# Counters set one stage ahead, batch 0's scores ahead of its layer norm, and a third of the slot table's lanes on ScalarE

## The reference

```python
x = x + xattn(layernorm(x), ctx)       # q, k = ctx @ Wq.T + bq, ctx @ Wk.T + bk
                                       # x + layernorm(x) mixed over channels by softmax(q k^T)
def ffn(x):                            # of layernorm(x); 4 batches of 512 tokens, width 512
    h = rmsnorm(x, ln1_w)
    x = x + causal_attention(h) @ wo   # 16 heads of 128
    h = rmsnorm(x, ln2_w)
    p = softmax(h @ gate_w.T)          # 16 experts, the 6 best of each token, weights made to sum to 1
    return x + routed(h, p) + shared(h)   # silu(h @ g) * (h @ u) @ d, width 352, shared 704
```

## Time and profile before

| | |
|---|---|
| runs, us | 2218.95, 2215.73, 2219.56 (median 2218.95) |
| profiled execution, us | 2220.62 |
| its span, first to last instruction | 2218.8 |
| PE busy | 2126.3 (96%) |
| DVE, POOL, ACT busy | 1146.1, 983.3, 699.4 |
| mean granted clock of PE | 0.985 |

### The profile page before, as it was taken

How to read it: one execution, slowest core, us unless ns; L and a number is a source line. 1 busy time by engine, 2 the same in 40 slices (tenths; PEclk the granted TensorE clock), 3 DMA queues, 4 the chain that set the end, 5 groups by cost and what they waited for, 6 DMA issues and landing times. The chain is left out here.

```text
span 2218.8 us, 39627 instructions
## 1 busy us (share of the span) xinstructions
PE 2126.3 (96%) x11850; PEld 1857.6 (84%) x11851; DVE 1146.1 (52%) x2520; ACT 699.4 (32%) x1832; POOL 983.3 (44%) x1036
## 2 busy tenths in 40 slices
PE   7899999999999999999996998889999999999997
PEld 5788888988888898888874876679999999999996
DVE  6746556464655646465566476633333333433332
ACT  6634334343433434343444211112222222222221
POOL 2535454545545454554515025534444444444442
PEclk9999999999999999999997999999999999999998
DMA  2214343443433344343415111086776776677443
GB/s 105 95 58 162 125 141 119 153 153 113 161 126 138 121 154 151 113 165 124 147 53 223 77 67 48 20 270 160 194 202 159 190 203 162 161 197 199 81 77 52
DMA packets 140690, 300.62 MB, mean 135 GB/s; under 512 B 16800, under 2 KB 16800, under 8 KB 138592
## 3 DMA queue, kind: packets, MB, share of 16 engines
q1 hardware_dynamic: 115392, 241.26, 30.6%
q0 software_dynamic: 24960, 58.21, 13.3%
q10 hardware_dynamic: 288, 0.53, 0.1%
HBM read 177.51 MB, written 122.42 MB: 135 GB/s over the span
## 5 line engine op out<-in xcount | busy, mean ns | idle before, releaser
L1094 POOL TENSOR_TENSOR chunk_hi<-chunk_raw,zero 128x512 fp32r<-128x512 f32 x153 | 159.3, 1041 | 239.9 <-DMA chunk_raw<-in_whole 239.9
L1975 POOL DMA_INDIRECT out<-y,sidx x111 | 177.4, 1598 | 62.8 <-issue 41.2
L1096 POOL TENSOR_TENSOR chunk_raw<-chunk_raw,chunk_hi 128x512 fp32r<-128x512 f32 x153 | 197.7, 1292 | 12.0
L1312 DVE TENSOR_TENSOR pT_lo<-ps,pT_hi 128x384 fp32r<-128x384 f32 (+2 forms) x256 | 111.2, 456 | 176.7 <-ACT pT_hi L1253 172.8
L2125 DVE TENSOR_TENSOR prod<-ps,silu 128x352 f32<-128x352 f32 x111 | 58.3, 525 | 271.6 <-PE ps L69 242.6
L1284 DVE SCALAR_TENSOR_TENSOR HS<-ps,rinv,HS 128x512 f32<-128x512 f32 x260 | 176.9, 743 | 2.8 <-PE ps L69 2.8
L1982 POOL TENSOR_TENSOR carry<-ident 128x1 f32<-128x1 f32 x214 | 42.6, 199 | 300.9 <-DVE gidx L2131 210.3
L1242 ACT ACTIVATE prob<-ps,negmax 128x512 f32<-128x512 f32 (+3 forms) x256 | 131.7, 527 | 110.1 <-DVE negmax L1273 110.1
L2120 DVE TENSOR_SCALAR y<-ps,weight_of 128x512 f32<-128x512 f32 x111 | 83.3, 751 | 136.3 <-PE ps L69 132.6
L67 PE MATMUL ps<-wv_or_qk_hi,hT_hi 128*128 128x256 f32 x512 | 146.4, 286 | 5.0 <-POOLq L1104 5.0
L67 PE MATMUL ps<-ring,xT_0hi 128*128 x448 | 150.2, 335 | 0.8 <-DMA ring<-split_weights 0.8
(11 more groups left out here) (320 smaller groups left out, 6064.7 us busy)
## 6 DMA issues: line engine op xcount, KB each, us to landing
ring<-split_weights SPq DMA_DIRECT2D x240, 272.0 KB
chunk_raw<-in_whole SPq DMA_DIRECT2D x153, 256.0 KB, 2.7
split_weights<-chunk_hi SPq DMA_DIRECT2D x153, 256.0 KB, 2.4
split_weights<-chunk_raw SPq DMA_DIRECT2D x153, 256.0 KB, 2.6
xg<-in_wqk SPq DMA_DIRECT2D x16, 512.0 KB, 3.6
x_spill<-x SPq DMA_DIRECT2D x4, 1024.0 KB, 4.1
xg<-in_wv SPq DMA_DIRECT2D x8, 512.0 KB, 3.4
xg<-in_wo SPq DMA_DIRECT2D x8, 512.0 KB, 5.1
```

Source lines behind the costliest of these rows:

```text
L1094: nc.gpsimd.tensor_tensor(chunk_hi[k][:], chunk_raw[k][:], zero[:].to_broadcast([P, CH]), ALU.add).then_inc(chunk_high, 1)
L1096: nc.gpsimd.tensor_tensor(chunk_raw[k][:].bitcast(F32R), chunk_raw[k][:], chunk_hi[k][:].bitcast(F32), ALU.subtract).then_inc(chunk_low, 1)
L1312: nc.vector.tensor_tensor(pT[1][:, 0:split, w], ps_t[k % 2][:, 0:split * P].rearrange("p (j t) -> p j t", t=P), pT[0][:, 0:split, w].bitca ...
L1975: nc.gpsimd.indirect_dma_start(out, bass.IndirectOffsetOnAxis(ap=sidx[q][:], axis=0), y[q][:], None, bounds_check=T + P - 1, oob_is_err=Tr ...
```

## The change

It does four things.

- The counters of `self_attention` (28 increments, `EARLY` and the three raised by 2 among them) are counted up by POOL at the start of `cross_attention`, and those of `routed_experts` (14) in `shared_expert`, between POOL's set-up and its wait for the packed slots. The first waits for `pool_0` of PE, ACT and DVE in `self_attention` and of PE in `routed_experts` are gone.
- In batch 0 of `cross_attention` PE makes the scores before it turns x, ACT takes queries and keys out of PSUM and splits the next features before it norms x, and copies the turned x between exponents and probabilities. Queries and keys of batch 1 wait for `dve_qk` instead of the four exponents, and x's tiles have other PSUM banks.
- The third lane of each batch is made by ACT in two instructions (`Abs` of lane minus count, then `Relu` of 1 minus that), at the end of each slot. PE waits for it with one wait more.
- In the slots c = 0 to 2 DVE makes the first column of a batch between `prod` and the low part, except for batch 0.

The earlier, unused copies of functions are deleted, which moves line numbers.

```diff
+            for counter in following:            # cross_attention, POOL, before of_x(0)
+                nc.gpsimd.sem_inc(counter, ONE)
+            for counter in following[0:2]:
+                nc.gpsimd.sem_inc(counter, EARLY)
+            for counter in following[2:5]:
+                nc.gpsimd.sem_inc(counter, 2)
             of_x(0)
...
-        banks = {("x", 0): B + C_, ("e", 0): D_ + A}
+        banks = {("e", 0): B + C_, ("x", 0): D_ + B}
...
-                    if n < 3:
+                    if n == 1:
+                        pe.wait_ge(dve_qk, 2)
+                    elif n == 2:
                         pe.wait_ge(act_exp, ST * n)
...
             keys_and_queries(0)
+            scores(0)
             normed_x(0)
-            scores(0)
...
             act.wait_ge(ld_b, 32)
+            high_qk1(0)
+            high_feat(1)
             layer_norm(0)
-            high_qk1(0)
-            high_of_tiles(columns(xT[0]), "x", 0)
             for n in range(NB):
-                if n + 1 < NB:
+                if 0 < n < NB - 1:
                     high_feat(n + 1)
...
-                softmax(n)
+                exponents(n)
+                if n == 0:
+                    high_of_tiles(columns(xT[0]), "x", 0)
+                probabilities(n)
...
             low_qk1(0)
-            low_of_tiles(*both(xT), "x", 0)
...
                 if n == 0:
+                    low_of_tiles(*both(xT), "x", 0)
                     statistics(1)
...
-            for counter in counters:             # self_attention and routed_experts, POOL
-                nc.gpsimd.sem_inc(counter, ONE)
...
-            pe.wait_ge(pool_0, 1)                # the same for act and dve
...
+            for counter in following:            # shared_expert, POOL
+                nc.gpsimd.sem_inc(counter, ONE)
             pool.wait_ge(dve_r, PACKED)
...
-                for b in range(RING):
+                for b in range(RING - 1):
                     r, t = divmod(RING * k + b, TT)
                     nc.gpsimd.tensor_scalar(in_lane[b][:], count[:], lane[:, t, r:r + 1], None, ALU.is_equal).then_inc(pool_lane, 1)
...
-                pe.wait_ge(pool_lane, RING * (k + 1))
+                pe.wait_ge(pool_lane, (RING - 1) * (k + 1))
+                pe.wait_ge(act_lane, 2 * (k + 1))
...
+            def last_lane(n, slot):
...
+                apart = in_lane[RING - 1]
+                nc.scalar.activation(apart[:], count[:], ACT.Abs, bias=lane[:, t, r:r + 1], scale=-1.0).then_inc(act_lane, 1)
+                act.wait_ge(act_lane, 2 * k + 1)
+                nc.scalar.activation(apart[:], apart[:].bitcast(F32), ACT.Relu, bias=1.0, scale=-1.0).then_inc(act_lane, 1)
...
+            ahead = lambda n, c: 1 if at_slot.get((n, c), 0) else 0
...
+                    columns(n, c, range(ahead(n, c)))
                     dve.wait_ge(act_h, q + 1)
...
-                    columns(n, c)
+                    columns(n, c, range(ahead(n, c), RING))
```

More of the change, by code:

```diff
@@ L124, in _ @@
                                     pattern=[[-1, P]], channel_multiplier=1).then_inc(made, 1)
-def high_qk(nc, qkT, corner, m, bank):
-    w, scale = slice(P if m == 0 else 0, S), SCALE if m == 0 else 1.0
-    nc.scalar.mul(corner[:, m, :], bank[:, 0:P], scale)
-    return nc.scalar.mul(qkT[0][:, m, w], bank[:, w], scale)
-def low_qk(nc, qkT, m, bank):
-    w = slice(P if m == 0 else 0, S)
-    return nc.vector.scalar_tensor_tensor(out=qkT[1][:, m, w], in0=bank[:, w], scalar=SCALE if m == 0 else 1.0,
-                                          in1=qkT[0][:, m, w].bitcast(F32), op0=ALU.mult, op1=ALU.subtract)
@@ L730, in attention @@
                     pe.wait_ge(act_nrm, ST * n + i + 1)
-                    if i == 0 and n >= 2:
+                    if n == 0:
+                        pe.wait_ge(dve_t, tile("x", 0) + i + 1)
+                    elif i == 0 and n >= 2:
                         pe.wait_ge(dve_t, tile("h", n - 2) + ST)
@@ L843, in softmax, with probabilities @@
                                          accum_out=rsum[:, i:i + 1]).then_inc(act_exp, 1)
+            def probabilities(n):
                 for i in range(ST):
@@ L996, in self_attention @@
         sb = lambda name, shape, dt=F32: ctx.enter_context(nc.sbuf_tensor(name, shape, dt))
-        counters, count = counting(sem)
         at = placing(nc, slab)
@@ L1713, in _ @@
         def _(act):
+            def last_lane(n, slot):
+                k = at_slot.get((n, slot))
+                if k is None:
+                    return
+                r, t = divmod(RING * k + RING - 1, TT)
+                if k == 0:
+                    act.wait_ge(dve_r, PACKED)
+                else:
+                    act.wait_ge(pe_table, k)
+                apart = in_lane[RING - 1]
+                nc.scalar.activation(apart[:], count[:], ACT.Abs, bias=lane[:, t, r:r + 1], scale=-1.0).then_inc(act_lane, 1)
+                act.wait_ge(act_lane, 2 * k + 1)
+                nc.scalar.activation(apart[:], apart[:].bitcast(F32), ACT.Relu, bias=1.0, scale=-1.0).then_inc(act_lane, 1)
             act.wait_ge(dve_r, LOGITS)
@@ L1731, in _ @@
                     nc.scalar.copy(hh[n % 2][0][0:w, c, :], prod[0:w, :]).then_inc(act_h, 1)
+                    last_lane(n, c)
+                if n >= 1:
+                    for i in range(ST):
+                        last_lane(n, NI + i)
         @block.vector
@@ L1837, in unit_tables, with columns @@
                 nc.vector.tensor_copy(base_of[:], ps_unit[:, 1, 0:UNITS])
-            def columns(n, slot):
+            def columns(n, slot, some=range(RING)):
                 k = at_slot.get((n, slot))
@@ L1847, in columns @@
                     dve.wait_ge(pe_table, k)
-                for b in range(RING):
+                for b in some:
                     r, t = divmod(RING * k + b, TT)
```

399 lines of the change are left out of this document (37 added, 362 removed).

## The result

The changed kernel takes 2204.43 us (median of 4 runs, 2203.29 to 2205.18) against 2219.26 of the kernel before beside it: ratio 0.9935, interval 0.9918 to 0.9952, or 14.8 us less where 13.4 were forecast. The profiled execution took 2203.29, with a span of 2201.4: 17.3 us under the profiled execution of before, and 3.9 under the 2207.2 that the prediction gave for it. The median lies near the forecast, the single profile less near, and the larger question of this study is what lies between the two.

A forecast was written before the change was run, and what follows sets the result against it. PE, busy nearly the whole span, was taken as the bound, its waits as the gain: 2.2 + 1.1 + 1.9 + 5.2 + 3.0 = 13.4, so 2218.95 - 13.4 = 2205.5 us, range 2200.5 to 2211.

The forecast's parts named there:

- Counters of the second stage: Second stage's start: without POOL's increments ahead of it PE starts at 128.6 instead of 130.80, 2.2 us gained (2.0 to 2.4).
- The cover: POOL's 10.64 us of idle time before its batch 0 deviations, to hide the 28 moved increments (2.2 us).
- Of the last stage: Last stage's start: 14 increments moved into POOL's waiting, so PE starts 1.1 us earlier (1.0 to 1.2).
- Batch 0: First stage: new order, DVE's list sets the end, scores of batch 1 start 1.9 us earlier (0.8 to 2.8).
- the 30.0: Forecast start in us of PE's scores of batch 1 in the first stage, instead of 31.93.
- Third lane: Down slots: POOL done earlier, DVE's columns last; 14 waits each 0.37 us shorter, 5.2 in all (2.8 to 5.9).
- The rival of table loads of ACT: Slots with ACT's lane: Abs and Relu each load a function table, 19 x 1.28 = 24.3 us, 2229.8; chance 0.02.
- The sign that the prediction named: ACT in the new kernel's profile: two table loads in all, if the forecast is right.
- Column in the gap: First down slot of steps 3 to 7: a column fits DVE's gap, 5 x 0.60 = 3.0 us (2.5 to 3.3).
- Clock: Second stage's start, batch 0, last stage's start: no gain counted, 1.3 us allowed either way for a 1.2 GHz stretch.
- POOL and VectorE: Table's columns: by the skill's page POOL contends with DVE for SBUF, so columns would shorten beside less POOL work.
- more than priced: Table and clock: shorter columns (14 x 0.05) and vanished low stretches (1.3 + 1.3) give 2202.2, down to 2200; chance 0.10.

The follow-up runs named there:

- the counters alone: Kernel before with only the counters of both stages set one stage ahead, nothing else of the change: 2216.22 us, ratio 0.9990.
- the second trace of the same kernel: The changed kernel profiled once more, not edited: median 2204.30 us, ratio 0.9935; the profiled execution took 2205.18.
- last slot alone: Changed kernel with DVE's column ahead of the low part only in the third slot (c == 2): 2204.37 us, ratio 0.9935.
- early slots alone: Changed kernel with DVE's column ahead of the low part only in the first two slots (c < 2): 2209.53 us, ratio 0.9957.

## Why the prediction was right

- **Counters of the second stage**: forecast 2.2, measured 2.1 by the idle time (5.04 to 2.94, 2.95 with the counters alone). The cover was there, and the start came as forecast. But by the hundredth matmul only 1.2 were left, since PE now works through more of the stretch of 0.50. The prediction asked whether the shorter idle time would save a stretch, and not whether the earlier start would meet more of it. **Of the last stage**: forecast 1.1, measured 1.2. Right.
- **Batch 0**: forecast 1.9; 0.9 to 2.0 by the time to the scores of batch 1, 2.4 by the medians (interval of the ratio from 1.6 permille less to none). Right by mechanism: DVE's list is the end. The size has luck in it. The 31.93 from which the forecast subtracts holds 1.4 us of low clock that the new order does not remove, and the 30.0 is too late. The scores began at 28.86, and at 29.42 in the second trace of the same kernel. Of this difference 0.6 is the clock at the start: the second bank of queries and keys was taken as ready at 15.29 from matmuls 0.43 apart, and in the first execution they were 0.23 apart from 13.8 on, so that ACT's copy started at 14.61. When the clock rises is no property of the kernel: 12.4 to 15.9 in fourteen traces, 13.8 and 15.8 in the two of the changed kernel.
- **Third lane**: forecast 5.2 (14 x 0.37), measured 6.0 in the table. Mechanism right, the term 0.8 small: the period fell to 2.85 and not to 2.9 (14 x 0.4 = 5.7), and the slots that wait for DVE gained a little. The rival of table loads of ACT is out: the two instructions take 0.40 and 0.31 us, 32 times each, with no load between. The Trainium skill says in "ScalarE: Activation LUTs" (Table sets) that relu and abs are in every set, and this trace agrees. The sign that the prediction named, two table loads in all, was there.
- **Column in the gap**: forecast 3.0, measured 2.8 alone and 3.0 beside the lane. The sum was right and the reason too (last slot alone keeps it, early slots alone lose it), but the place where it would be seen was wrong. The prediction had the wait at the first down slot fall from 1.13 to 0.5. It named the four waits one slot ahead and put them at no gain, which is right, but did not follow them: they go away as well, which brings PE to the first down slot by as much earlier, and the wait there stays at 1.12 to 1.14. Only in step 3, without a wait at the slot ahead, did it fall (1.44 to 0.81).
- **Clock**: "I count nothing, and allow 1.3 either way at each". This was the mis-sized step. The stretches of 1.2 GHz in batches 1 to 3 of the first stage, on which I did not count at all, were 0 to 10.2 us long in executions of the same code, and moved the end of the stage by up to 4.6 us (4.2 when counted from PE's first matmul). The profile undercut its forecast by 3.9: the first stage ended 4.8 earlier where 1.9 was forecast, and the table gave 9.0 where 8.2 was. The median's gain is 14.8 where 13.4 was forecast. What the traces show as lasting is 1.2 + 1.2 + 0.9 to 2.0 + 9.0, or 12.3 to 13.4, which the interval of the measured gain, 10.7 to 18.2, holds. That the median came so near owes something to misses that offset each other.
- **POOL and VectorE**: that columns would get shorter beside POOL's shorter work did not show: 1.91 for three, before and after. The profile's time lies in the range of the case "more than priced", but by the clock and not by this.

## What to carry to other kernels

Compare two kernels by intervals between the same instructions (first to last product of a table, first matmul to a batch's scores) before comparing ends: here the table's repeated within 0.1 us where the whole moved by 2 to 6 with the clock, and one profile of each kernel would have credited an edit with 4.8 us that brought 2.0 at most. The interval must hold the same work on both sides: one that six matmuls had moved into showed 4.8 us for a gain of 6.2. A shorter idle time is not yet a gain either: 2.1 us less of it left 1.2 a hundred matmuls later. When a wait on a chain is shortened, ask where the chain starts, and which engine passes two waits of it: only the last one counts, and the earlier can vanish without a gain. A fixed chain can be hidden by moving the waiter's own work in front of the wait: six matmuls there gave 6.2 us, twice the column in the gap.

## What the hardware showed that was not expected

- One idle time of 2.42 us in the first stage was followed by 0, 3.5, 7 or 10 us of granted clock 0.50 (1.2 GHz) in executions whose PE work there was the same.
- In the table's part the clock stayed up behind waits of 1.12 to 1.14 us, four in each of the changed kernel's two traces, and behind 1.44 us before. It fell behind two of the four waits of 1.72 to 1.74. So a slightly longer wait can cost up to twice its length: in that trace 3.0 us of waits came to 5.8.
- At the second stage's start both kernels have a stretch of granted clock 0.50. Starting PE 2.1 us sooner after its idle time began put 28 matmuls into the first 6 us, where before there were 35, and took back 0.9 us.
- Filling the idle time with matmuls kept the clock at 1.00 at both stage starts, in both kernels that did it, and the second stage's first 47 matmuls took 5.7 us, where 28 had taken 6.0. The stage's hundredth came 2.6 us sooner.
